# Order of loads, stores and ScalarE's pieces for the second image, in a convolution and matrix kernel on one core

## The reference

```python
t1 = p1_w * x                                  # p1_w: a factor for each channel and row
t2 = x + t1
t4 = jax.nn.relu(x)
t5 = _unfold(x, 3, 7, 1, 1, 1, 3)              # 21 shifted copies
t7 = jnp.einsum('oc,nchw->nohw', p7_w, t4)
t8 = _unfold(t7, 1, 5, 1, 3, 0, 6)             # 5 copies, 3 columns apart
t9 = x[:, :, None] - t8
t10 = jnp.einsum('ngihw,goi->ngohw', xg, wg).reshape(n, c * 21, h, w)   # xg, wg: t2, p10_w in 4 groups
t11 = jnp.einsum('nck,nmk->ncm', t1f, t5f) / math.sqrt(h * w)
t12 = t9.mean(2)
t13 = jnp.einsum('ncm,nmk->nck', t11, t10.reshape(n, c * 21, h * w))
t13 = t13.reshape(n, c, h, w) / math.sqrt(c * 21)
return jnp.maximum(t13, t12)
```

## Time and profile before

| what | value |
|---|---|
| median of 3 runs | 395.06 us (395.03 to 396.93) |
| the profiled execution | 392.89 us, its span 391.1 us |
| busy: PE, DVE, ACT, POOL | 382.6 (98%), 330.9 (85%), 254.1 (65%), 91.6 (23%) us |
| chain that ended last | PE 84%, DVE 6%, DMA 5%, ACT 2% |
| DMA | 88.80 MB, mean 227 GB/s; queue 1's packets 64.4% of 16 engines' span |

### The profile page before, as it was taken

One profiled execution on the slowest core, in us unless ns is written; L12 is line 12 of the kernel. 1 busy time (PEld: TensorE's weight loads), 2 busy tenths in 40 slices (PEclk: granted clock), 3 DMA queues, 4 the chain that ended last, 5 costly groups with the idle time before them and its releaser, 6 DMA issues.

```text
span 391.1 us, 10230 instructions
## 1 busy us (share of the span) xinstructions
PE 382.6 (98%) x4022; PEld 172.2 (44%) x4022; DVE 330.9 (85%) x400; ACT 254.1 (65%) x721; POOL 91.6 (23%) x77
## 2 busy tenths in 40 slices
PE   7999999989999999999999999999999999999996
PEld 3233563353833347333653337433373334732383
DVE  7998999999788896888968888788868889688645
ACT  3425478579577683777656773777827768377790
POOL 1634200822022212222022220222202222122300
DMA  8999116983977757775667937779377783453115
GB/s 294 372 367 415 38 50 260 390 316 111 315 258 256 270 175 238 264 261 196 200 220 252 334 116 224 228 271 318 125 262 238 246 305 110 158 195 109 54 56 215
DMA packets 28704, 88.80 MB, mean 227 GB/s; under 512 B 3312, under 2 KB 3824, under 8 KB 28656
## 3 DMA queue, kind: packets, MB, share of 16 engines
q1 hardware_dynamic: 28656, 88.14, 64.4%
HBM read 71.35 MB, written 16.78 MB: 225 GB/s over the span
## 4 chain that ended last, share of the span: by engine, by line
PE 84%; DVE 6%; DMA 5%; ACT 2%; issue 1%; SPq 0%; DVEq 0%; ACTq 0%
PE ps_y L811 37%; PE ps_y L910 13%; PE ps_t L833 11%; PE ps_p L833 11%; PE ps_y L822 8%; DMA out<-base 3%; DMA xw<-x_conv 2%; DVE pair_sum L635 2%; PE ps_y L1055 1%; DVE box L643 1%; ACT t L398 1%; PE ps_y L833 1%; PE ps_t L811 0%; DVE v_planes L564 0%; DVE v_planes L559 0%
## 5 line engine op out<-in xcount | busy, mean ns | idle before, releaser
L811 PE MATMUL ps_y<-v_planes,u_planes 64*64 64x512 f32 x1488 | 184.1, 594 | 0.4 <-DVE v_planes L564 0.3
L290 POOL TENSOR_TENSOR t1T<-t1T,p1T_sb 128x512 f32<-128x512 f32 x64 | 84.4, 1341 | 267.6 <-PE ps_y L822 212.1
L398 ACT ACTIVATE t<-xn,p_plus 128x64 f32<-128x64 f32 x512 | 127.9, 335 | 0.0
L833 PE MATMUL ps_t<-t,aT 64*64 64x512 f32 x440 | 113.3, 590 | 0.1
L833 PE MATMUL ps_p<-box,p_fifth 64*64 64x512 f32 x424 | 109.0, 589 | 2.5 <-ACT ps_p L322 2.5
L811 PEld LDWEIGHTS ps_y<-v_planes,u_planes 64*64 64x64 f32 x1488 | 56.8, 133 | 110.7 <-issue 103.7
L625 DVE STREAM_TRANSPOSE yT<-ps_y 128x512 f32<-128x512 f32 x62 | 40.7, 695 | 30.5 <-PE ps_y L822 30.1
L322 ACT ACTIVATE base<-ps_p 128x512 f32<-128x512 f32 x55 | 32.8, 596 | 50.6 <-PE ps_p L833 45.9
L910 PEld LDWEIGHTS ps_y<-t1T,yT 128*128 128x128 f32 x448 | 50.5, 192 | 5.7 <-issue 5.7
L910 PE MATMUL ps_y<-t1T,yT 128*128 128x128 f32 x448 | 51.9, 277 | 0.0
L659 DVE TENSOR_TENSOR base<-ps_t,base 128x512 f32<-128x512 f32 x56 | 38.4, 687 | 12.2 <-PE ps_t L833 11.9
(11 more groups left out here) (74 smaller groups left out, 221.0 us busy)
## 6 DMA issues: line engine op xcount, KB each, us to landing
xw<-x_conv SPq DMA_DIRECT2D x63, 561.0 KB, 6.6
xn<-x_nat SPq DMA_DIRECT2D x32, 512.0 KB, 4.5
t1T<-x_pix SPq DMA_DIRECT2D x32, 512.0 KB, 5.0
out<-base SPq DMA_DIRECT2D x63, 256.0 KB, 4.8
u_planes<-w_tiles SPq DMA_DIRECT2D x4, 336.0 KB, 6.2
out<-base SPq DMA_DIRECT2D x2, 128.0 KB, 2.0
p1T_sb<-p1T SPq DMA_DIRECT2D x1, 128.0 KB, 7.6
p_sb<-p7T SPq DMA_DIRECT2D x1, 64.0 KB, 7.7
```

Source lines behind the costliest of these rows:

```text
L290: nc.gpsimd.tensor_tensor(part, part, p1T_sb[:, e, :].unsqueeze(1).broadcast_to([P, 4, C]), ALU.mult).then_inc(t1_ready, 1)
L398: last = nc.scalar.activation(t2[:, h, W * r:W * (r + 1)], xn[:, f, at:at + W], ACT.Copy, scale=p1_plus[:, 8 * h + r:8 * h + r + 1])
L811: last = nc.tensor.matmul(dst[TILE * pair:TILE * pair + TILE, :], weights_of(rows_of(half), u, weights, TILE * k, TILE), data_of(rows_of(h ...
L833: last = nc.tensor.matmul(dst[cols, 0:data.shape[-1]], weights[rows, cols], data[rows, :], start=start, stop=False, skip_group_check=True)
```

## The change

In SyncE's list the loop over images begins one image later, and the entries of image 1 (groups 7 to 10, its x_nat and t1T, the first four stores) stand written out in another order. In ScalarE's list t2_half(0, 4) stands behind base_half(0, 5) and seed_x(0, 6). The first memset, of relu_pad's second buffer (16 rows of 76), becomes two: 7 rows and 9 rows; TensorE's zero products read the first 7 rows (532 columns, of which they use 512) and wait for that memset alone.

```diff
+ZERO_ROWS = 7
...
             load_group(6)
-            for n in range(1, N_IMG):
+
+            load_group(7)
+            load_group(8)
+            load_natural(1, 0)
+            load_pixels(1, 0, 2)
+            load_group(9)
+            load_pixels(1, 2, 4)
+            load_natural(1, 1)
+            store(0, 0)
+            load_natural(1, 2)
+            store(0, 1)
+            store(0, 2)
+            load_natural(1, 3)
+            load_group(10)
+            store(0, 3)
+            for n in range(2, N_IMG):
                 u = GROUPS * n
                 load_group(u + 3)
...
             copy_two(5)
             relu(1, 0)
             t2_half(0, 3)
-            t2_half(0, 4)
             base_half(0, 5)
             seed_x(0, 6)
+            t2_half(0, 4)
             t2_half(0, 5)
             base_half(0, 6)
             seed_x(0, 7)
...
-            nc.vector.memset(relu_pad[:, 1], 0.0).then_inc(zeroed, 1)
+            nc.vector.memset(relu_pad[:, 1, 0:ZERO_ROWS], 0.0).then_inc(zeroed, 1)
+            nc.vector.memset(relu_pad[:, 1, ZERO_ROWS:], 0.0).then_inc(zeroed, 1)
             nc.vector.memset(relu_pad[:, 0], 0.0).then_inc(zeroed, 1)
...
             pe.wait_ge(zeroed, 1)
-            zeros = relu_pad[:, 1].rearrange("p a b -> p (a b)")
+            zeros = relu_pad[:, 1, 0:ZERO_ROWS].rearrange("p a b -> p (a b)")
```

## The result

Six executions of each kernel on one chip, taken in turn: 389.86 us after (389.45 to 391.8), 395.28 before (393.85 to 396.93). The ratio is 0.987, its 95% interval 0.984 to 0.990.

What follows compares the result with a forecast made beforehand. TensorE, 98% busy, was held up by two mid-kernel waits for ScalarE's seed. Terms -1.04 - 2.07 - 0.06 + 0 = -3.17 us took the median from 395.06 to 391.9 us, range 390.9 to 394.0.

Steps and rivals of the forecast that it cites:

- (1): ScalarE's list: t2_half(0, 4) behind copy and seed makes the seed usable by 61.7; -1.04 us in group 6's slot.
- Wait (A): Group 6's slot: TensorE waits for ScalarE's seed, held behind sixteen rows of t2 from 58.35; 1.04 us.
- (2): SyncE's new order: first store issued at 61.2, home by 73.1, before base_half(1, 0) wants it at 75.2; -2.07 us.
- Wait (B): Group 8's slot: TensorE waits for the seed behind base_half(1, 0), held until 78.65 by image 0's first store; 2.07 us.
- (3): GpSimd and VectorE: earlier t1T separates multiplies from plane differences, putting max_half(0, 3) at 75.9; TensorE wants it at 77.0.
- (4): Start: split first memset ends TensorE's zeros about 0.5 us sooner, first real product unchanged; 0 us, bounds +0.3 and -0.57.
- the second: VectorE becomes the bound in groups 6 to 8; 0.6 to 1.7 us come back, say 393.0; chance 0.13.
- third: Group 8's wait for the store stays in part, through another condition or load; 393.4 to 394.0 us; chance 0.07.
- The fifth: Start: earlier zeros leave TensorE idle, its clock rises later, real products run at half speed; up to 399.7; chance 0.04.
- The fourth rival: Change fails in the timed executions, 2.2 us longer than the profiled one for an untraceable reason; about 395; chance 0.06.
- K: Theory formed during experiments: TensorE's granted clock falls during group 8's wait, and products behind it run at half rate awhile.
- S: Experiments' theory: group 8's wait is longer in timed executions because the store lands later, costing 2.2 us more than 2.07.

Runs made afterwards that it cites:

- e7: Kernel before with store(0, 0) alone moved ahead of image 1's t1T pieces and group 9's planes: 393.2 us, ratio 0.996.
- e9: Changed kernel with image 1's four t1T pieces loaded behind store(0, 0) again: 390.96 us, ratio to before 0.991.
- e3: Kernel before with only the first memset split and the zero products reading its first part: 394.35 us, ratio 0.999.
- e4: Changed kernel without its earlier zeros (SyncE order and t2 row move only): 389.91 us, ratio 0.986 to before.
- e1: Kernel before with SyncE's new order of image 1's loads and stores alone: 390.64 us, ratio 0.989.
- e8: Kernel before with two useless zero-weight products on TensorE ahead of the seed awaited in group 8's slot: 394.02 us, ratio 0.998.
- e12: Kernel before, unchanged, profiled again (last of three): 393.61 us, granted clock 1.000.
- e10: Kernel before, unchanged, profiled again (first of three): 397.31 us, granted clock 0.996.
- e5: Changed kernel with eight needless ScalarE copies ahead of base_half(1, 0), making TensorE wait without a store: 391.63 us.
- e11: Kernel before, unchanged, profiled again (second of three): 396.8 us, granted clock 0.995.
- e6: Changed kernel with eleven needless ScalarE copies ahead of base_half(1, 0), making TensorE wait without a store: 394.82 us.
- e2: Kernel before with t2_half(0, 4) alone moved behind base_half(0, 5) and seed_x(0, 6): 395.91 us, ratio 1.001.

## Why the prediction was right, and where it was wrong

**Right, step by step.** (1) Wait (A) went whole, with copy and seed at 60.15 and 60.87; slot 6 lost 1.06 us for a forecast 1.04. (2) Wait (B) went whole; the issue times on SyncE up to the first store came within 0.2 us (the second store at 66.64 for 66.8, the third 0.6 us sooner than forecast, at 70.9), the copy at 75.16 for 75.2; slot 8 lost 2.06 us for 2.07, slot 9 the 0.06. (3) That the earlier t1T is needed, as max_half(0, 3) "would now be late", was shown twice: in e7 it took the store's place with 1.0 us of wait, and in e9 it cost 1.14 us of slot 8. The Trainium skill (SBUF — State Buffer, section "SBUF: two separate sides") gives the lock between GpSimd and a VectorE instruction with two SBUF inputs; the slow pairs of e9 agree, 2.07 against 1.22 us for a box sum and 1.79 against 0.72 for planes. (4) The zeros gave nothing: e3 at 0.999 of before, e4 (389.91) beside after (389.86). The memsets ended at 3.39 us, sooner than the 3.65 forecast, and neither bound (+0.3, -0.57) shows in these medians. Of the rivals, the second and third stayed away after the change. The fifth, a clock that rises late at the start, stayed away too: in the profiled execution real products ran 24 in 3.12 us from 7.60, 0.13 us each, against 0.12 in the earlier trace rows. One reading of the prediction was loose: not all the loads went out together from 60.65. By SyncE's order and timeline before, the third piece of x_nat and group 9's planes stand behind the t1T pieces; they were issued at 65.33 and 65.70, just ahead of the store at 66.66. The conclusion, that the store queued behind them, stands.

**Wrong.** The step that failed is one sentence of the change's part: the sum is put "on the median shown, 395.06, which lies 2.17 us higher; I assume that this offset stays." It didn't. It is not a fixed cost of timing: the changed kernel's offset is 0.17 us. So wait (B), put at 2.07 us, was mis-sized: that was its cost in one execution, and a short one. In the median the loads and stores in their new order are worth 4.1 us (e1). The low end of 390.9 had room only for the zeros and some scatter. The offset splits as follows, from the second set (before 394.95, the first profile 392.89, so 2.06). These are differences of medians, and uncertain: the interval of e8's ratio alone is 1.7 us wide.

- 0.93 us (394.95 less 394.02, e8): the granted clock falls to 0.50 behind the wait in about 4 of 10 executions (26 of 64), and these are 1.2 us longer in the median (395.31 less 394.07). The profile read had a clock of 1.00 throughout, so it showed none of it.
- 0.82 us (394.02 less 393.2, e7): the rest of the difference between a wait on a late store and one on VectorE. Slot 8 was at its best in the first profile (11.92, and 11.96 in e12), and e3 had 12.84 with the clock at 1.00 and 11.02 of it busy: the products behind the wait came apart, as in e9. That this is the whole of the 0.82 was not tested, and losses ahead of slot 6, which e10 to e12 show, were not measured apart in the timed executions.
- 0.31 us is left (393.2 less 392.89). It is near the 0.17 that the changed kernel's median has over its own profiled execution.

The fourth rival had named the offset, "for a reason that the trace can't show", but took it for something that might cancel the change, not as part of what the change removes. The fifth had named the clock, but only for the start. The trace shown held the hint for K: two waits of TensorE of up to 1.7 us, in a kernel whose timed executions spread over 2 us and lay above the profiled one.

**Half-misses in the experiments.** K alone expected lowered clocks behind the 1.6 us of e5, and there were none. S alone was expected to explain the missing part through the store's landing time. The landing times hardly vary (11.69 to 12.31 us in seven profiles with the old order). What varies is what follows the wait: whether the clock holds, and whether the products stay side by side; and, apart from the wait, what is lost ahead of slot 6.

## What to carry to other kernels

When the timed executions lie above the profiled one, don't carry the difference over as a constant: ask which wait could be its source, and profile the kernel before two or three times more, since one profile may be its best case. A wait of TensorE can cost more than its length, because the clock may fall behind it: here it did behind some waits of 1.8 to 2.0 us and most of 3 us or more. A shorter wait in its place can be a gain in the median that one profile doesn't show (e7: 1.75 us against none). And look at busy time per slot as well as at waits: a result that came 0.7 us late cost 1.14 us here with no wait in any list.

## What the runs showed of the hardware that was not expected

- TensorE's granted clock fell in the middle of a kernel that keeps it 98% busy: to 0.50 (1.2 GHz) behind waits of 1.84 and 1.99 us (e10, e11), not behind waits of 1.77 (e12) and 1.82 (e3), and in none of eight executions with 1.6 us (e5); behind 3.1 us in eight of twelve (e6), with the row of t2 moved alone (3.4 us) in ten of twelve. The same kernel does it in some executions and not in others (the kernel before in 26 of 64). The Trainium skill (TensorE: Matmul & The Clock Gate, section "What's actually happening") says of the clock's rise that its moment varies from run to run, because it isn't tied to the kernel's start. These runs show a scatter of the fall, which such a cause would explain, but none tests it; no run here shows the moment of the rise at the start.
- Once down, it stayed at 0.50 from about 80 to 86.6 us in e2, though TensorE was busy from 80.86 on.
- With two zero products in the gap (e8) the clock held in twelve of twelve executions; without them it was lowered in 12 of 31 in the same set.
- A store of 256 KB queued behind 4.8 MB of loads landed after 11.7 to 12.3 us in all seven profiles with the old order; with one load in front of the first of them (the profile after), the stores issued up to 90 us took 2.0 to 6.3.
